# Eight chunks of gathered rows fetched row by row from SyncE, and count rows fetched for two nodes per transfer, in a graph network kernel

## Chip, cores and metric

One core of a Trainium2 chip runs the whole kernel. The time is the device time of one execution in microseconds, and the figure compared is the median over runs. A profiled execution adds a trace of every engine: TensorE (PE, its weight loads apart as PEld), VectorE (DVE), ScalarE (ACT), GpSimd (POOL) and SyncE (SP).

## What is computed

A residual layer on a graph of 12,500 nodes (64 features) and 200,000 edges that are sorted by their target node `dst`; `src` is random.

```python
h = relu(layernorm(x))
m = relu(concat(h[src], h[dst]) @ W1 + b1) @ W2 + b2   # 200000 edges, hidden size 128
s = segment_sum(m, dst)                                # one sum per node
out = x + s / max(count(dst), 1)
```

## The kernel before

**Tables first.** `h @ W1` splits into a part for the source and a part for the target. Until about 200 us the kernel writes both for all nodes to memory: `p_table` (source part, 128 floats, 512 bytes a row) and `q_table` (target part with the bias).

**The main loop.** Edges are cut into 391 quads of 512 edges (4 chunks of 128, one edge per partition). Two quads make a couple, and the loop of `fast()` runs over 182 couples, `m` = 0 to 181, on every engine, each in its own program order. A round is what an engine does for one `m`. For a couple:

- POOL fetches the source rows: one indirect DMA per chunk, 128 rows of `p_table` into one column block of tile `g` (L672 in `gather`), so 8 per couple. `g` is a ring of 26 quads, 13 couples. POOL waits once per two couples, on `u_psum` (couples that PE has finished), and then issues the next 16 indirect DMAs without another wait. How many quads it may be ahead shrinks by 4 every 48 quads, from 26 to 8 (`ahead`).
- ACT or DVE makes `spreads` (which target row belongs to which edge) and `member` (the reverse), from rows that SP broadcasts from `rel_table` (L556).
- PE adds the target part and the source part in PSUM tile `z`: `spread_q` (L1374) for couple m + 1, `add_rows` (L1386) for couple m. ACT applies relu (L812, `r_done`), PE sums the edges by node (`sum_edges`, L1401, `u_psum`), multiplies by `W2` (L1408, L1419) and DVE adds the result to the sums (L1100). In PE's program round m is: `add_rows(m)`, `times_w2` for couple m - 2, `dense(m)`, `spread_q(m + 1)`, `sum_edges(m)`.

**The dense nodes.** The first 28 quads belong to 68 nodes with very many edges, and are done another way. In rounds 3 to 42 a table of counts per source node is made (`tally_table`, stored by SP at L563). From round 49 to round 174 DVE multiplies, for each of 13 spans of 1024 source nodes and each of the 68 dense nodes, a PSUM tile (`turned`) with a row of counts (L1153, `product_of`), 6 or 7 products a round. SP brings each row of counts, broadcast to 128 partitions, 256 KB a time (L584, `load_tallies`), into one of 6 buffers, and waits until the product that used the buffer is done (`product_done`). In SP's program the rows for DVE's round m - 2 stand in round m.

**SP's program order** in a round is: `rel_table` rows (even rounds), the windows of `q_table` (L551, whose address comes from `base_i` through registers, L460), the rows of counts, and at a few rounds rows of `p_table` for a new span or stored results. A wait in it holds back all that stands behind it.

Of the kernel before, what the change touches and what calls it, by code (L numbers as in the profile page):

```python
# [8 lines left out]
I32 = mybir.dt.int32  # L9
# [153 lines left out]
BUFFERS = 6  # L163
# [30 lines left out]

MEAN_AT_OF = [BLOCK_END[k] + 2 for k in MEAN_BLOCK]
# [3 lines left out]
assert DENSE <= BT * NP and MEAN_AT_OF[0] < COUPLES  # L199
# [7 lines left out]
def gnn_kernel(nc, x, src, dst, W1, b1, W2, b2, out):  # L207
# [6 lines left out]
    with ctx:  # L214
# [60 lines left out]
        base_i = sb("base_i", [1, QT * 128], I32)  # L275
# [32 lines left out]
        tally_row = [above_ring(512 * k, 512, U16) for k in range(BUFFERS)]  # L308
        product = [above_ring(512 * k, 512, BF16) for k in range(BUFFERS)]
        p_rows = above_ring(3072, 1024, F32).rearrange("p (j h) -> p j h", h=HID)  # L310
# [69 lines left out]
        tally_in = [sem(f"tally_in{k}") for k in range(BUFFERS)]  # L380
# [71 lines left out]

        def rows_landed(m):

            rounds, k = divmod(m, RING // 2)
            return 128 * (rounds - (2 * k < RAW)) + 16 * chunks_in(m)
# [41 lines left out]
        def _(sp):  # L498
# [80 lines left out]
            def load_tallies(i, k, d):  # L579
                if i >= BUFFERS:  # L580
                    sp.wait_ge(product_done, i - BUFFERS + 1)
                row = HIGH_DIGITS * d + SPAN // 512 * k
                digits = -(-span_of(k) // 512)
                sp.dma_start(tally_row[i % BUFFERS][:, 0:512 * digits],  # L584
                             tally_table[row:row + digits, :].rearrange("(o a) b -> o (a b)", o=1)
                             .to_broadcast([128, 512 * digits])).then_inc(tally_in[i % BUFFERS], 16)
# [49 lines left out]
        def _(pool):  # L636
# [22 lines left out]
            def gather(n):  # L659
# [11 lines left out]
                for j in range(chunks_of(n)):  # L671
# [212 lines left out]
        def _(dve):  # L884
# [173 lines left out]
            nc.vector.tensor_copy(base_i[:, :], base[0:1, :]).then_inc(windows, 1)  # L1058
# [190 lines left out]
        def _(pe):  # L1249
# [318 lines left out]
```

## Time and profile before

| | |
|---|---|
| median of 3 runs | 2845.76 us (2832.94 to 2848.27) |
| profiled execution | 2839.25 us |
| its span | 2837.4 us |
| around the span | 1.85 us |
| busy: PE, DVE, POOL, ACT | 1548.3, 1428.9, 1372.7, 1189.8 us |
| mean granted TensorE clock | 0.75 of full |
| before the main loop | about 200 us |

The span runs from the first to the last instruction. No engine is busy more than 55% of it, so busy time alone does not tell what sets the time: the waits do. In every view, time stands in microseconds from the start of the span; `[11.06 <-PE bank L1401]` behind an instruction means that its engine was idle 11.06 us before it and that PE's line 1401 released it. "issue" means that nothing the profile shows was waited for, "remote" that the releaser was not found.

### The profile page before, as it was taken

Reading aid. Unit: us, or ns where it says so; the run is one execution under the profiler, and the core shown is the slowest. Engines: PE = TensorE matmul, PEld = TensorE weight load, DVE = VectorE, ACT = ScalarE, POOL = GpSimd, SP = SyncE. Lnnn points to the kernel's source line nnn. Section 1 sums busy time; section 2 is a strip of 40 time slices with the busy share of each in tenths; the row PEclk is TensorE's granted clock in tenths of the full one; section 3 lists DMA queues with packets and bytes.
Section 4 is the critical chain, followed back from the end, with each engine's and each line's share of the span. In section 5 each row is a group of like instructions: output and inputs, shape, how many; then the busy total and the mean of one; then the engine's idle time right before and its main releaser. Section 6 shows DMA issues by size and latency. Waiting matters only on the chain.

```text
span 2837.4 us, 26976 instructions
## 1 busy us (share of the span) xinstructions
PE 1548.3 (55%) x8249; PEld 1183.2 (42%) x8250; DVE 1428.9 (50%) x3051; ACT 1189.8 (42%) x2414; POOL 1372.7 (48%) x1460
## 2 busy tenths in 40 slices
PE   1656565566465564455544555455455545555556
PEld 0545353444344443344433444344344434434444
DVE  3554343343324665456655666456565556655421
ACT  1223343444314544345444454344344444444444
POOL 6345545445555445444554435545544554554553
PEclk6878777788787777677776777767776777776778
DMA  4532222222134656556565566556565665665541
GB/s 90 163 109 60 59 61 59 60 59 58 58 98 144 202 181 189 167 169 200 179 192 154 178 188 200 186 159 183 184 192 168 186 191 174 183 186 157 174 119 43
DMA packets 258990, 408.46 MB, mean 144 GB/s; under 512 B 45128, under 2 KB 118749, under 8 KB 258841
## 3 DMA queue, kind: packets, MB, share of 16 engines
q1 hardware_dynamic: 211845, 312.84, 35.7%
q0 software_dynamic: 46432, 93.61, 12.5%
q8 instruction: 68, 1.11, 0.2%
q14 instruction: 81, 0.66, 0.1%
q10 hardware_dynamic: 564, 0.23, 0.0%
HBM read 388.12 MB, written 18.38 MB: 143 GB/s over the span
## 4 chain that ended last, share of the span: by engine, by line
PE 48%; issue 36%; another core or an unknown queue 9%; DVE 6%; ACT 1%; DMA 0%; DVEq 0%; SPq 0%; ACTq 0%
PE z L1374 16%; PE bank L1401 12%; PE z L1386 10%; DVE g L1153 4%; PE bank L1419 2%; PE bank L1408 2%; PE z L1445 2%; PE bank L1430 1%; PE z L1461 1%; DVE rows_b L936 1%; PE bank L1268 1%; DVE norms L920 1%; PE z L1268 1%; ACT g L812 0%
## 5 line engine op out<-in xcount | busy, mean ns | idle before, releaser
L672 POOL DMA_INDIRECT g<-p_table,src_e x1403 | 1326.1, 945 | 1425.3 <-PE bank L1401 960.5
L1153 DVE SCALAR_TENSOR_TENSOR g<-z,norms,g 128x1024 bf16<-128x1024 f32 (+1 forms) x884 | 1019.1, 1214 | 43.5 <-issue 25.3
L812 ACT ACTIVATE g<-z 128x1024 f32<-128x1024 f32 x182 | 185.6, 1020 | 1468.0 <-remote 1153.5
L1100 DVE TENSOR_TENSOR acc<-acc,bank 65x128 f32 x191 | 54.2, 284 | 1201.0 <-remote 1069.7
L1374 PE MATMUL z<-work 128*128 128x128 f32 x1464 | 258.8, 348 | 514.2 <-issue 482.9
L1374 PE MATMUL z<-w,work 128*128 128x128 f32 x1438 | 251.9, 345 | 484.3 <-issue 443.8
L1374 PEld LDWEIGHTS z<-work 128*128 128x128 f32 x1464 | 240.3, 256 | 546.0 <-issue 541.7
L1374 PEld LDWEIGHTS z<-w,work 128*128 128x128 f32 x1438 | 234.4, 253 | 512.3 <-issue 509.3
L1401 PE MATMUL bank<-work,g 128*128 128x128 f32 x2902 | 423.4, 307 | 15.4 <-issue 15.1
L1401 PEld LDWEIGHTS bank<-work,g 128*128 128x128 f32 x2902 | 414.1, 227 | 16.8 <-issue 16.7
L1386 PE MATMUL z<-g,ident 128*128 128x512 f32 x726 | 350.8, 605 | 5.8 <-issue 5.7
L803 ACT ACTIVATE work<-columns,rel_e 128x128 f32<-128x128 f32 x1059 | 324.2, 396 | 0.0
L1386 PEld LDWEIGHTS z<-g,ident 128*128 128x128 f32 x726 | 126.0, 194 | 98.7 <-issue 98.7
L796 ACT ACTIVATE work<-work 128x1024 f32<-128x1024 f32 (+1 forms) x168 | 146.5, 872 | 4.2
L808 ACT ACTIVATE work<-work 128x1024 f32<-128x1024 f32 (+1 forms) x133 | 140.0, 1053 | 4.2
L825 ACT ACTIVATE g<-g,norms 128x512 bf16<-128x512 f32 x157 | 108.3, 716 | 0.0
L1445 PE MATMUL z<-g 128*125 128x512 bf16 x236 | 65.6, 409 | 70.6 <-remote 67.3
L1419 PE MATMUL bank<-sums_u,w 128*64 128x128 f32 (+1 forms) x312 | 78.7, 326 | 33.3 <-issue 33.3
L830 ACT ACTIVATE g<-g 128x512 bf16<-128x512 bf16 x157 | 93.5, 620 | 0.0
L1408 PE MATMUL bank<-ident,count 128*1 128x128 f32 x432 | 74.5, 273 | 9.5 <-issue 9.4
L1408 PEld LDWEIGHTS bank<-ident,count 128*1 128x1 f32 x432 | 23.4, 81 | 128.3 <-issue 125.2
L788 ACT ACTIVATE work<-rel_q,rows_f 128x1024 f32<-128x1024 bf16 (+1 forms) x67 | 75.3, 1124 | 0.0
(161 smaller groups left out, 1063.6 us busy)
## 6 DMA issues: line engine op xcount, KB each, us to landing
g<-tally_table SPq DMA_DIRECT2D x816, 256.0 KB
rel_q<-rel_table SPq DMA_DIRECT2D x46, 512.0 KB
rows_b<-rel_table SPq DMA_DIRECT2D x45, 512.0 KB
g<-p_table,src_e POOLq DMA_INDIRECT x1403
g<-tally_table SPq DMA_DIRECT2D x68, 128.0 KB
work<-q_table SPq DMA_DIRECT2D x96, 64.0 KB
w<-q_table SPq DMA_DIRECT2D x96, 64.0 KB
g<-p_table SPq DMA_DIRECT2D x12, 512.0 KB
```

Source lines behind the costliest of these rows:

```text
L672: nc.gpsimd.indirect_dma_start(out=g[:, slot(n), j * HID:(j + 1) * HID], out_offset=None, in_=p_table, in_offset=bass.IndirectOffsetOnAxis ...
L796: nc.scalar.activation(to, to, ACT.Relu, bias=1.0, scale=-1.0, accum_out=count[:, j:j + 1])\
L803: last = nc.scalar.activation(member[:, m % 2, c, :], columns[:, :], ACT.Abs, bias=rel_e[:, NC + 8 * m + c:NC + 8 * m + c + 1], scale=-1.0)
L808: nc.scalar.activation(to, to, ACT.Relu, bias=1.0, scale=-1.0)
L812: nc.scalar.activation(rows_of_p(m), z[:, 0:HID * chunks_in(m)], ACT.Relu).then_inc(r_done, 1)
L1153: nc.vector.scalar_tensor_tensor(product[i % BUFFERS][:, 0:w], turned[:, 0:w], minus_q[:, d:d + 1], tally_row[i % BUFFERS][:, 0:w], ALU.ma ...
L1374: last = nc.tensor.matmul(z[:, at:at + HID], spreads[m % 2][:, at:at + 128], qw[i % WINDOWS], start=c == 0, stop=False)
L1386: last = nc.tensor.matmul(z[:, 512 * (n % 2):512 * (n % 2) + w], ident[:, :], g[:, slot(n), 0:w], start=False, stop=True)
L1401: last = nc.tensor.matmul(u_bank[k % 2][:, at:at + WIN], g[:, slot(n), HID * c:HID * (c + 1)], member[:, m % 2, 4 * (n % 2) + c, :], start ...
L1408: nc.tensor.matmul(v[FEAT:FEAT + 1, at:at + WIN], count[:, j % COUNTS:j % COUNTS + 1], ident[:, :], start=j == parts[0], stop=j == parts[-1])
L1419: nc.tensor.matmul(v_of(k)[0:FEAT, 0:w], w2[:, :], sums_u[:, k % 2, 0:w], start=True, stop=True).then_inc(v_psum, 1)
L1445: last = nc.tensor.matmul(tally_bank[i % 2][0:125, :], high_hot[p % TALLY_PLACES], low_hot[p % TALLY_PLACES], start=p == TALLY_FIRST[i], s ...
```

## The change

Two things are changed, both in what SP issues.

**Rows of P one by one.** For eight couples (26, 46, 66, ..., 166) POOL no longer fetches the last chunk of the couple's second quad. SP does: it loads the 128 source numbers of that chunk at the start of `fast()` (eight small transfers and one wait), and in rounds c - 10 to c of couple c it loads 12 numbers into registers and issues 12 transfers of one row of 512 bytes each (8 in the last round). Before the first of a chunk it waits until couple c - 13, which used the same place of the ring, is finished by PE. PE's `add_rows` of the eight couples waits for these rows too. POOL's indirect DMAs in the main loop fall from 1347 to 1339 in the program; SP's program grows from 800 to 3095 rows of the listing below.

**Count rows in pairs.** One transfer brings the rows of counts of two nodes (512 KB); 442 in place of 884. The buffers grow from 6 to 8, and DVE waits on one semaphore for a pair. SP issues a pair for products i and i + 1 when product i - 7 is done. Where rows of P are issued too, they stand between the pairs.

SP's program where the main loop starts; before:

```order
L467 TENSOR_LOAD widest [waits q_pad,q_out3,windows,q_out2,widest_done,q_out1,q_out0]
L467 ISA x2
L468 COMPARE_AND_BRANCH
L556 DMA rel_q<-rel_table 128x2048 [waits rel_out]
L460 TENSOR_LOAD base_i
L551 ISA
```

and after:

```order
L498 TENSOR_LOAD widest [waits q_pad,q_out3,windows,q_out2,widest_done,q_out1,q_out0]
L498 ISA x2
L499 COMPARE_AND_BRANCH
L623 DMA base_i<-in_src_dram 1x128x1 x2
L623 DMA base_i<-in_src_dram 1x128 x6
L587 DMA rel_q<-rel_table 128x2048 [waits row_src_in,rel_out]
L491 TENSOR_LOAD base_i
```

Eight transfers and a wait for their landing (`row_src_in`) now stand ahead of the first row of `rel_table`.

SP's program in round 76, in the stage with products; before:

```order
L556 DMA rel_q<-rel_table 128x2048 [waits spread_done]
L460 TENSOR_LOAD base_i
L551 ISA [waits zq_done]
L551 DMA work<-q_table 128x128
L584 DMA g<-tally_table 128x1024 [waits product_done] x7
```

and after, where `u_psum` waits for couple 73:

```order
L587 DMA rel_q<-rel_table 128x2048 [waits spread_done]
L491 TENSOR_LOAD base_i
L582 ISA [waits zq_done]
L582 DMA work<-q_table 128x128
L632 TENSOR_LOAD base_i [waits u_psum]
L614 DMA g<-tally_table 128x2x1024 [waits product_done]
L642 ISA
L642 DMA g<-p_table 1x128
L642 ISA
L642 DMA g<-p_table 1x128
```

All rows of counts of the round, which stood behind `product_done` alone, now stand behind a wait for PE; 12 row transfers, each with an instruction that sets its address, are spread between them.

The core of the diff:

```diff
-BUFFERS = 6
+BUFFERS = 8
+ROW_FIRST, ROWS_EARLY, ROWS_LATE = 16, 12, 12
+def row_chunks():
+    m, chunks = ROW_FIRST, []
+    while True:
+        rows, rounds = 0, []
+        while rows < 128:
+            more = min(ROWS_EARLY if m < PRODUCT_ROUND else ROWS_LATE, 128 - rows)
+            rounds.append((m, range(rows, rows + more)))
+            rows, m = rows + more, m + 1
+        if m >= COUPLES - 1:
+            return chunks
+        chunks.append((m - 1, rounds))
+        m += 9
...
+        two_rows = [above_ring(1024 * k, 1024, U16).rearrange("p (d s) -> p d s", d=2) for k in range(BUFFERS // 2)]
...
+        def gathers_in(n):
+            return chunks_of(n) - (couple_of(n) in ROW_COUPLES and n == couple(couple_of(n))[-1])
...
             def load_tallies(i, k, d):
                 if i >= BUFFERS:
-                    sp.wait_ge(product_done, i - BUFFERS + 1)
...
+                    sp.wait_ge(product_done, i - BUFFERS + 2)
+                w = 512 * -(-span_of(k) // 512)
+                sp.dma_start(two_rows[i % BUFFERS // 2][:, :, 0:w],
...
+            def load_row_src(i):
...
+                sp.dma_start(row_src[i], edges[c:c + 1, :], allow_slow_non_contiguous=n < 128).then_inc(row_src_in, 16)
+            def row_nodes(m):
+                if m not in ROW_AT:
+                    return []
+                i, rows = ROW_AT[m]
+                if rows[0] == 0:
+                    sp.wait_ge(u_psum, ROW_COUPLES[i] - RING // 2 + 1)
+                _, nodes = nc.values_load_multi_w_load_instructions(
...
+            def load_node_rows(m, nodes):
+                for p, node in nodes:
...
+                    sp.dma_start(g[p:p + 1, slot(n), HID * c:HID * (c + 1)], p_table[bass.ds(node, 1), :])\
+                        .then_inc(row_in[i % 2], 16)
             def dense(m):
+                nodes = row_nodes(m)
...
-                for k, d in products_in(m - 2):
+                twos = [(k, d) for k, d in products_in(m - 2) if d % 2 == 0]
+                for j, (k, d) in enumerate(twos):
                     load_tallies(DENSE * k + d, k, d)
+                    load_node_rows(m, nodes[len(nodes) * j // len(twos):len(nodes) * (j + 1) // len(twos)])
+                if not twos:
+                    load_node_rows(m, nodes)
...
             def fast():
                 stores = 0
+                for i in range(len(ROW_CHUNKS)):
+                    load_row_src(i)
                 sp.wait_ge(rel_out, 16)
+                sp.wait_ge(row_src_in, 16 * len(ROW_CHUNKS))
...
-                for j in range(chunks_of(n)):
+                for j in range(gathers_in(n)):
...
-                dve.wait_ge(tally_in[i % BUFFERS], 16 * (i // BUFFERS + 1))
+                dve.wait_ge(tally_in[i % BUFFERS // 2], 16 * (i // BUFFERS + 1))
...
+                if m in ROW_COUPLES:
+                    i = ROW_COUPLES.index(m)
+                    pe.wait_ge(row_in[i % 2], 16 * 128 * (i // 2 + 1))
```

## Rows read from the trace of the kernel before

**Rows 1.** The page, part 5 (busy, mean ns, idle before): POOL's indirect DMAs.
```profile
L672 POOL DMA_INDIRECT g<-p_table,src_e x1403 | 1326.1, 945 | 1425.3 <-PE bank L1401 960.5
```
**Rows 2.** The waits, longest first: us in total, times, longest us.
```profile
ACT g L812 <- remote: 1153.5, 83, 15.6
DVE acc L1100 <- remote: 1069.7, 82, 21.7
...
POOL g L672 <- PE bank L1401: 960.5, 84, 27.9
...
POOL g L672 <- issue: 400.8, 1315, 0.3
...
DVE g L1153 <- DMA g<-tally_table: 13.1, 17, 1.6
```
**Rows 3.** The timeline, 1213 to 1247 us: start, us, engine, line.
```profile
1213.76 0.94 POOL L672 DMA_INDIRECT g<-p_table,src_e  x1 [11.06 <-PE bank L1401]
1215.01 0.94 POOL L672 DMA_INDIRECT g<-p_table,src_e  x1 [0.30 <-issue]
...
1232.48 0.94 POOL L672 DMA_INDIRECT g<-p_table,src_e  x1 [0.30 <-issue]
1236.56 1.02 ACT L812 ACTIVATE g<-z 128x1024 f32<-128x1024 f32 x1 [14.49 <-remote]
...
1237.45 1.28 DVE L1153 SCALAR_TENSOR_TENSOR g<-z,norms,g 128x1024 bf16<-128x1024 f32 x1 [0.46 <-issue]
...
1237.68 3.75 PE L1374 MATMUL z<-work 128*128 128x128 f32 x16 [15.11 <-issue]
...
1241.22 2.96 PE L1401 MATMUL bank<-work,g 128*128 128x128 f32 x16
...
1244.46 0.94 POOL L672 DMA_INDIRECT g<-p_table,src_e  x1 [11.03 <-PE bank L1401]
```
**Rows 4.** The timeline of PE inside a burst of gathers, 2761 to 2770 us.
```profile
2761.91 0.27 PE L1401 MATMUL bank<-work,g 128*128 128x128 f32 x1 [1.74 <-issue]
...
2769.69 0.59 PE L1401 MATMUL bank<-work,g 128*128 128x128 f32 x2 [1.73 <-issue]
```
**Rows 5.** Busy time by stretch; behind POOL's: granted clock, DMA share, GB/s.
```profile
1212.70:1226.20 13.50, 9.38 (x55) 6.00 (x54) 10.77 (x19) 6.76 (x14) 9.44 (x10) 1.00 0.86 262
1226.30:1243.30 17.00, 5.62 (x26) 5.65 (x27) 6.13 (x10) 6.68 (x14) 5.60 (x6) 0.50 0.34 104
```
**Rows 6.** The timeline of POOL: first gather of six bursts that follow one another.
```profile
2323.06 0.94 POOL L672 DMA_INDIRECT g<-p_table,src_e  x1 [11.06 <-PE bank L1401]
...
2352.24 0.94 POOL L672 DMA_INDIRECT g<-p_table,src_e  x1 [9.51 <-PE bank L1401]
...
2382.07 0.94 POOL L672 DMA_INDIRECT g<-p_table,src_e  x1 [10.16 <-PE bank L1401]
...
2412.33 0.94 POOL L672 DMA_INDIRECT g<-p_table,src_e  x1 [10.58 <-PE bank L1401]
...
2442.83 0.94 POOL L672 DMA_INDIRECT g<-p_table,src_e  x1 [10.82 <-PE bank L1401]
...
2473.40 0.94 POOL L672 DMA_INDIRECT g<-p_table,src_e  x1 [10.89 <-PE bank L1401]
```
**Rows 7.** The timeline of SP: a transfer of one row, and the loop's start.
```profile
22.41 0.25 SPq L506 DMA_DIRECT2D acc<-in_src_dram  x1
...
201.16 0.37 SPq L556 DMA_DIRECT2D rel_q<-rel_table  x1
```
**Rows 8.** The timeline of all engines at the loop's start: DVE.
```profile
204.56 1.28 DVE L1081 TENSOR_SCALAR_CACHE_REDUCE work<-rel_q,rows_f 128x1024 f32<-128x1024 bf16 x1 [0.94 <-DMA rel_q<-rel_table]
```
**Rows 9.** The timeline of SP, round 76 with its neighbours.
```profile
1217.89 0.43 SPq L556 DMA_DIRECT2D rel_q<-rel_table  x1
...
1219.47 5.61 SPq L584 DMA_DIRECT2D g<-tally_table  x6
...
1238.77 9.77 SPq L584 DMA_DIRECT2D g<-tally_table  x7
```
**Rows 10.** The waits of SP's queue: us in total, times, longest us.
```profile
SPq L584 <- DVE g L1153: 1048.0, 441, 14.9
```

More of the change, by code:

```diff
@@ L192, in span_of @@
     return SPAN if k < SPANS - 1 else TAIL
+ROW_FIRST, ROWS_EARLY, ROWS_LATE = 16, 12, 12
[11 more added lines that the diff above has]
+        m += 9
+ROW_CHUNKS = row_chunks()
+ROW_COUPLES = [m for m, _ in ROW_CHUNKS]
+ROW_AT = {m: (i, rows) for i, (_, rounds) in enumerate(ROW_CHUNKS) for m, rows in rounds}
+assert len(ROW_CHUNKS) <= 24 and ROW_COUPLES[0] >= RING // 2
 MEAN_AT_OF = [BLOCK_END[k] + 2 for k in MEAN_BLOCK]
@@ L198 @@
     MEAN_AT_OF[0] += 1
-assert DENSE <= BT * NP and MEAN_AT_OF[0] < COUPLES
+assert DENSE % 2 == 0 and DENSE <= BT * NP and MEAN_AT_OF[0] < COUPLES
 ORDER = sorted(range(BATCHES), key=lambda b: MEAN_AT_OF[b])
@@ L274, in gnn_kernel @@
         base = sb("base", [128, QT * 128])
-        base_i = sb("base_i", [1, QT * 128], I32)
+        base_i = sb("base_i", [128, QT * 128], I32)
+        places = [(k, q) for k in (base_i, real[:, :].bitcast(I32)) for q in (32, 64, 96)]
+        row_src = [k[q:q + 1, 128 * i:128 * (i + 1)] for k, q in places for i in range(4)]
         idx_raw = sb("idx_raw", [128, 4 * RAW], I32)
@@ L308, in gnn_kernel @@
         tally_row = [above_ring(512 * k, 512, U16) for k in range(BUFFERS)]
+        two_rows = [above_ring(1024 * k, 1024, U16).rearrange("p (d s) -> p d s", d=2) for k in range(BUFFERS // 2)]
         product = [above_ring(512 * k, 512, BF16) for k in range(BUFFERS)]
-        p_rows = above_ring(3072, 1024, F32).rearrange("p (j h) -> p j h", h=HID)
+        p_rows = above_ring(512 * BUFFERS, 1024, F32).rearrange("p (j h) -> p j h", h=HID)
         parts_d = norms[:, 0:SPANS * DENSE].rearrange("p (d k) -> p d k", k=SPANS)
@@ L379, in gnn_kernel @@
             "p_rows_in turned_done product_done edges_psum added_done v_dense_psum dense_added dense_range")
-        tally_in = [sem(f"tally_in{k}") for k in range(BUFFERS)]
+        row_src_in = sem("row_src_in")
+        row_in = [sem(f"row_in{k}") for k in range(2)]
+        tally_in = [sem(f"tally_in{k}") for k in range(BUFFERS // 2)]
         o_psum, most_done, inverse_done, mean_done, out_done = sems("o_psum most_done inverse_done mean_done out_done")
@@ L451, in rows_of_p @@
             return g[:, k:k + 2, :].rearrange("p k c -> p (k c)")[:, 0:HID * chunks_in(m)]
+        def gathers_in(n):
+            return chunks_of(n) - (couple_of(n) in ROW_COUPLES and n == couple(couple_of(n))[-1])
         def rows_landed(m):
-            rounds, k = divmod(m, RING // 2)
-            return 128 * (rounds - (2 * k < RAW)) + 16 * chunks_in(m)
+            first = m % (RING // 2) + (RING // 2 if 2 * (m % (RING // 2)) < RAW else 0)
+            return 16 * sum(gathers_in(n) for c in range(first, m + 1, RING // 2) for n in couple(c))
         def first_nodes(eng, n):
@@ L580, in load_tallies @@
                 if i >= BUFFERS:
-                    sp.wait_ge(product_done, i - BUFFERS + 1)
[L582 to L586, printed above, removed]
+                    sp.wait_ge(product_done, i - BUFFERS + 2)
+                w = 512 * -(-span_of(k) // 512)
+                sp.dma_start(two_rows[i % BUFFERS // 2][:, :, 0:w],
+                             tally_table.rearrange("(o d a) b -> o d (a b)", o=1, a=HIGH_DIGITS)[:, d:d + 2, SPAN * k:SPAN * k + w]
+                             .to_broadcast([128, 2, w])).then_inc(tally_in[i % BUFFERS // 2], 16)
+            def load_row_src(i):
+                n = couple(ROW_COUPLES[i])[-1]
+                at, c = n * QE, chunks_of(n) - 1
+                edges = src[at:at + QE].rearrange("(e c) -> c e", c=4) if n < 128 else \
+                    src[at:at + QE].rearrange("(c e) -> c e", c=4)
+                sp.dma_start(row_src[i], edges[c:c + 1, :], allow_slow_non_contiguous=n < 128).then_inc(row_src_in, 16)
[6 more added lines that the diff above has]
+                _, nodes = nc.values_load_multi_w_load_instructions(
+                    row_src[i][:, rows[0]:rows[-1] + 1], engines=[sp.engine], min_val=0, max_val=NODES - 1,
+                    skip_runtime_bounds_check_because="src holds nodes")
+                return list(zip(rows, nodes))
+            def load_node_rows(m, nodes):
+                for p, node in nodes:
+                    i = ROW_AT[m][0]
+                    n = couple(ROW_COUPLES[i])[-1]
+                    c = chunks_of(n) - 1
+                    sp.dma_start(g[p:p + 1, slot(n), HID * c:HID * (c + 1)], p_table[bass.ds(node, 1), :])\
+                        .then_inc(row_in[i % 2], 16)
             def dense(m):
+                nodes = row_nodes(m)
                 if m == TALLY_ROUND - 3:
@@ L1057, in _ @@
             nc.vector.tensor_copy(spans_i[:, :], bank[1][0:1, :]).then_inc(span_done_i, 1)
-            nc.vector.tensor_copy(base_i[:, :], base[0:1, :]).then_inc(windows, 1)
+            nc.vector.tensor_copy(base_i[0:1, :], base[0:1, :]).then_inc(windows, 1)
             for t in range(QT):
```

## Prediction

> **What bounds the kernel now.** I read the page's costliest groups first, then the waits, then the timeline of one cycle. POOL's indirect DMAs are 1326.1 us busy, 945 ns each, with 1425.3 us idle before them [rows 1]. The waits say that both sides wait: POOL waited 960.5 us in 84 waits for PE's `sum_edges`, and ACT's relu waited 1153.5 us, 83 times, for a release that was not found [rows 2]. About 84 long waits in 182 couples is one per two couples, so the timeline of two couples is the thing to see [rows 3]. POOL starts a burst of 16 gathers at 1213.76; starts are 1.25 us apart (945 ns and 0.30 of issue), and the last begins at 1232.48 and ends at 1233.42, so a burst is 19.66 us. ACT's relu of couple 73 (counted from the first of L812) begins at 1236.56, 3.14 us after the burst's end, having waited 14.49. Then comes PE: `spread_q` of couple 74 from 1237.68 (3.75 us), `sum_edges` of couple 73 from 1241.22 (2.96 us), and at 1244.46 POOL is released into its next burst. The cycle is 19.66 + 3.14 + 7.90 = 30.70 us.
>
> What PE waits for in it is not the burst's data: the burst that starts at 1213.76 fetches couples 79 and 80 by the count of L672. PE simply comes forward very little while POOL issues. In one late burst, where PE has nothing else to wait for, its matmuls stand singly with gaps of about 1.7 us [rows 4], where 16 of them take 3 us outside. Why is not shown; that the two take turns is. So POOL's gather time is on the path nearly whole, although POOL is idle half of the time. DVE and SP are not on it: DVE waited 13.1 us for count rows in all [rows 2], and SP waited 1048.0 us for DVE's products [rows 10].
>
> **The change, part by part.**
>
> *Eight gathers fewer on POOL.* Each takes 1.25 us out of a burst (15 in place of 16): 8 x 1.25 = 10.0 us. Nothing hides a burst's end, so I take all of it; the ends are 0 (something restores the cycle) and what follows.
>
> *The clock.* In a cycle the granted clock is at 2.4 GHz for the stretch around the burst's start and at 1.2 GHz from its middle until the next one is near (1.00 and 0.50) [rows 5]; PE had been idle before it fell and had worked for some us before it rose. PE's 6.7 us after a burst are mostly done at the low level. A cycle that comes out early is followed by more short ones: the burst at 2352.24 came 29.18 us after the one before, the next after 29.83, 30.26, 30.50 and 30.57, where 30.70 is usual [rows 6]. The shortfalls are 1.52 + 0.87 + 0.44 + 0.20 + 0.13 = 3.16 us, so a cycle early by 1.52 us gave 1.64 more in the cycles behind it. A burst shorter by 1.25 us then gives 1.6 more (the same sequel) to 1.9 (the same total). I expect it in the stage of products, where the cycles are steady and six of the eight chunks lie, and not in all of them: 4 x 1.6 to 4 x 1.9 = 6.4 to 7.6 us, taken 7. The ends are 0 and 8 x 1.9 = 15.
>
> *The start.* Eight small transfers and the wait for their landing stand ahead of the first row of `rel_table`, which is issued at 201.16 [rows 7], and DVE waited for its landing until 204.56 [rows 8]: it is on the path, nothing covers it. A transfer of one row took SP 0.25 us to issue [rows 7], with the gap 0.3; two of the eight pick single numbers and may take 0.5. That is 2.8 us of issue, and the landing of the last is bounded by the 3.4 us from issue to use of the first `rel_table` rows (4.56 - 1.16, a far larger transfer) and 1 us. Sum +3.8 to +6.2, taken +4.8.
>
> *1024 row transfers on SP.* Each has an instruction for its address. By the row of 0.25 us and two gaps and the register work (0.15) it costs 0.42 us of SP: 12 are 5.0 us a round. The trace has no one-row transfer with a register address; the nearest from above are the windows of `q_table` at 0.56 us [rows 9], so 6.7 us. A round lasts 30.7 / 2 = 15.4 us, and SP now waits 1048.0 us over 126 product rounds, 8.3 us a round [rows 10]. It fits, and costs 0 on the path. If it did not, SP would be late with count rows, which is the second rival.
>
> *The wait for couple c - 13 ahead of a chunk.* Behind it on SP stand the count rows of that round and all later ones. Round 76's are issued from 1219.47 [rows 9] for products that start at 1237.45 [rows 3]; now they wait for couple 73, whose `sum_edges` ends at 1244.2. With a load of registers (0.6) and about 3 us to land, DVE's round 74 starts at 1248, 10.5 us late, six times. Who waits: `add_sums` behind those products, and PE's `times_w2` behind that, which stands in round 75 inside the next burst, where PE stands still until 1267. DVE waited 1069.7 us in 82 waits at `add_sums` [rows 2], 13 us a cycle, so 10.5 fits, narrowly. Cost 0, at most 3 us in the two chunks (146, 166) whose waiting couple is released in mid cycle: 0 to +6, taken +2. The first two chunks have no count rows behind the wait: 0. The last rows of a chunk are issued in SP's round c. Round 76 was issued by 1225.08 [rows 9], and PE's `add_rows(76)` stands behind the relu of couple 75, one cycle after 1236.56: 42 us of lead, so the wait on the rows themselves costs 0.
>
> *Count rows in pairs.* 442 issues of 0.33 to 0.5 us in place of 884 of 0.37: SP gains about 1 us a round, the bytes are the same. The first product of a pair needs 512 KB landed, but it is requested six products (7.3 us) ahead as before. DVE waited 13.1 us for count rows in all, so at best that much is won on an engine with slack: 0.
>
> A page of the Trainium skill, "DMA: Bandwidth & Descriptors", section "Rules for kernel authors", speaks against this: many small transfers are to be coalesced, since below 64 KB the overhead is most of what is paid, and section "Anatomy of one DMA" gives about 2.0 us fixed for each. Laid end to end that would be an estimated 24 us a round of 12 rows, over the 15.4 of a round, and the chunks' 88 rounds would add some 760 us. The trace speaks for overlap: six transfers of 256 KB were issued in 5.61 us [rows 9], so I give a serial landing of the rows a chance of 0.01.
>
> Sum against the profiled execution (2839.25, of which 1.85 lies around the span): - 10.0 - 7 + 4.8 + 2 = - 10.2, so 2829.1. The median shown is 6.5 us above that execution; the middle of all four times is 2842.5, which would give 2832.3. I say **2831**.
>
> **Rivals.**
>
> *B, the burst is shorter and nothing else comes of it.* If the cycle falls back to 30.70 after each, only the direct 10.0 is left: - 10.0 + 4.8 + 2 = - 3, so 2838 to 2840. For it: most cycles are 30.7 whatever small work is in them, and six rows of one event are all I have for the follow-up.
>
> *C, no gain at all.* PE's progress after a burst may hang on the clock's next rise and not on the burst's end; then a burst that ends 1.25 us sooner changes nothing. + 4.8 + 2 over the base: 2847. For it: the cycle is very regular, POOL's idle time before its bursts is 11.06, 11.03 and again 11.06 us [rows 3, 6]. Against it: the shortfalls of rows 6. The same page of the Trainium skill (section "Issuing engines are not separate DMA queues") says that moving a transfer to another engine saves only the sequencer's time, since all run on the same 16 DMA engines. By it nothing is won but POOL's own 1.25 us; rows 3 say that this is just the time PE waits for.
>
> *D, slower: SP comes too late with the count rows.* The mechanism: the wait for couple c - 13, then 12 rows a round, make DVE late by more than the 13 us it idles, and PE waits for DVE at `times_w2` and at the change of a span. It decides at about 0.7 us a row: round 76 would then need 8.4 + 3 us, DVE's two rounds would end at about 1270, past 1267, and the lateness comes back each cycle of the chunk until SP has its lead again. Price: 3 to 5 us in each of six chunks at the start and 1 us in each of 5 cycles, 6 x 9 = 54 at worst, 30 as its likely size: 2842.5 - 10 + 4.8 + 30 = 2867. For it: 0.56 us on some rows of `q_table`. Against it: 0.25 for the one-row transfer.
>
> **How the numbers follow.** Forecast 0.42, B 0.24, C 0.15, D 0.16, something else 0.03 (the serial landing in it). The forecast's own range is 2818 to 2838: all gains at their upper ends, 2842.5 - 10 - 15 + 3.8 = 2821, and from the profiled execution 2818; without most of the sequels 2838. To leave out no more than 2 in 10, the range goes from 2816 over B and C to the near end of D: 2816 to 2858. A measurement of this kernel can tell about 0.5% from no change, 14 us: below 2831.5 is faster, above 2860 slower. About half of the forecast's spread lies below 2831.5, but both times come from the same session and the base may be lower: faster 0.38, same 0.45, slower 0.17.
>
> **What would show it.** Right: eight bursts with 15 gathers, 1.25 us shorter, in the timeline of POOL; the cycle after them below 30.7; DVE's first operation on the rows of `rel_table` at 209 in place of 204.56; PE's `add_rows` of the eight couples without a wait of its own; row transfers on SP of 0.3 us each; POOL's wait for PE about unchanged. Wrong: cycles of 30.7 with 15 gathers and a longer pause after them (C); DVE waiting for count rows tens of us in all, or PE's `times_w2` later than the relu it used to precede (D); a loop start that has not moved, which would give 5 us back.

## The result, and the profile after

The changed kernel takes 2904.76 us (median; 2898.61 to 2907.78), the kernel before 2845.85 in the same session: a ratio of 1.021, 95% interval 1.019 to 1.0231. The forecast was 2831. The change costs 59 us.

The groups of the page and the waits, of the kernel after (rows 1, 2 and 10 are those of before; L737 was L672, L1218 was L1153, L1469 was L1401, L614 was L584):

```profile
L737 POOL DMA_INDIRECT g<-p_table,src_e x1395 | 1319.3, 946 | 1498.4 <-PE bank L1469 1032.4
```

```profile
ACT g L877 <- remote: 1115.8, 79, 18.5
POOL g L737 <- PE bank L1469: 1032.4, 83, 40.9
...
DVE acc L1165 <- remote: 708.3, 55, 22.2
DVE g L1218 <- DMA g<-tally_table: 445.3, 89, 23.0
```

POOL issues eight gathers fewer and is 6.8 us less busy, but its idle time has grown by 73.1 us. The wait that has appeared is DVE's for count rows: 445.3 us in 89 waits, where it was 13.1 in 17 [rows 2]. Most of it came out of DVE's old idle time (1069.7 to 708.3), but not all of it. The next fence is SP's queue (issue times; a row's transfer is L642):

```profile
SPq L614 <- DVE g L1218: 427.0, 141, 15.4
...
SPq L632 <- PE bank L1469: 161.1, 6, 32.3
```

SP waits 621 us less for DVE than before [rows 10], though the new wait for couple c - 13 takes only 161.1 of that in the product stage. Most of the rest is SP's own time on the rows. SP's timeline of the fourth chunk, inside a burst that runs from 1299.73 to 1319.4, and then outside one (start, us, engine, line, transfers):

```profile
1302.39 4.48 SPq L642 DMA_DIRECT2D g<-p_table  x4
1306.88 0.70 SPq L614 DMA_DIRECT2D g<-tally_table  x1
1309.74 11.25 SPq L642 DMA_DIRECT2D g<-p_table  x4
1322.38 0.00 SPq L582 DMA_DIRECT2D w<-q_table  x1
...
1333.03 1.54 SPq L642 DMA_DIRECT2D g<-p_table  x4
1334.62 0.40 SPq L614 DMA_DIRECT2D g<-tally_table  x1
1335.21 1.46 SPq L642 DMA_DIRECT2D g<-p_table  x4
```

Four rows take 1.5 us outside a burst and, in the middle of one, over 11. The view of the line tells why. It lists the three instructions of a row, with the shortest, median and longest duration in ns:

```profile
L642 SPq FUSED_REGOPS  x1024: 2/37/1395, 403.1 to 2657.7; - x171
L642 SPq MOVE g<-p_table x1024: 1/29/1387, 403.2 to 2657.8; - x171
L642 SPq DMA_DIRECT2D g<-p_table x1024: 1/228/1396, 403.3 to 2657.8; - x171
```

A register addition and a move have nothing to wait for. Normally they take 37 and 29 ns; inside a burst most take 0.70 us or near nothing (339 and 256 of 691), like the other SP instructions there: SP comes forward by about one instruction per 0.70 us. This begins some 3 us behind the burst's first gather and ends some 3 us behind its last, which is about when the relu begins that waits for PE [rows 3]. Counted over the trace, some 290 of the 1024 rows lie inside such a stretch and cost SP 2.2 us each (mean, start to start of what follows); the others cost 0.45 (median 0.41). The mean is 0.95.

What it leads to, in the order of the chain (all engines, 1327 to 1361 us):

```profile
1327.56 1.28 DVE L1218 SCALAR_TENSOR_TENSOR g<-z,norms,g 128x1024 bf16<-128x1024 f32 x1 [13.56 <-DMA g<-tally_table]
...
1345.84 1.94 PE L1529 MATMUL z<-ident,g 128*128 128x128 f32 x8 [7.52 <-DVE g L1218]
...
1355.04 1.02 ACT L877 ACTIVATE g<-z 128x1024 f32<-128x1024 f32 x1 [15.88 <-PE z L1454]
...
1360.25 0.94 POOL L737 DMA_INDIRECT g<-p_table,src_e  x1 [40.85 <-PE bank L1469]
```

DVE waits 13.56 us for count rows that SP issued late, PE waits for DVE's product at the change of a span (L1529), the relu comes late, and POOL's burst starts 60.5 us after the one before, where 45.3 is usual at that place (there POOL skips a burst). Four more such gaps, each in another chunk and ahead of a burst's first gather (11.0 is usual, 9.5 to 10.9 behind a short cycle):

```profile
1055.43 0.94 POOL L737 DMA_INDIRECT g<-p_table,src_e  x1 [20.48 <-PE bank L1469]
...
1672.77 0.95 POOL L737 DMA_INDIRECT g<-p_table,src_e  x1 [18.77 <-PE bank L1469]
...
2256.91 0.94 POOL L737 DMA_INDIRECT g<-p_table,src_e  x1 [21.04 <-PE bank L1469]
...
2574.35 0.94 POOL L737 DMA_INDIRECT g<-p_table,src_e  x1 [21.67 <-PE bank L1469]
```

Burst by burst against the trace before: nine long cycles in the product stage, less one short one, cost 63.5 us together (15.2 at most, at 1360.25), the first burst comes 9.8 us later (233.01 against 223.22), the stage before the products adds 7.8, and the short bursts give back 14.6 in the product stage. That is 66.5, the difference of the two spans (2903.9 and 2837.4).

### The profile page after: what moved, and what is told of

It is laid out like the page before. It is cut to its first block, busy times and chain, and to the rows that moved or that the text cites. A ratio compares the mean times of both kernels' runs of the same rounds, so it can differ in the third digit from the quotient of the medians.

```text
span 2903.9 us, 29703 instructions
## 1 busy us (share of the span) xinstructions
PE 1580.4 (54%) x8249; PEld 1192.1 (41%) x8250; DVE 1430.4 (49%) x3051; ACT 1190.1 (41%) x2414; POOL 1365.9 (47%) x1452
## 4 chain that ended last, share of the span: by engine, by line
PE 33%; issue 33%; another core or an unknown queue 11%; SPq 10%; DVE 7%; DMA 5%; ACT 2%; DVEq 0%; ACTq 0%
PE z L1439 11%; PE bank L1469 8%; SPq L642 7%; PE z L1454 7%; DMA g<-tally_table 5%; DVE g L1218 4%; PE z L1513 2%; PE bank L1476 1%; PE bank L1487 1%; SPq L614 1%; SPq L582 1%; SPq L632 1%; DVE rows_b L1001 1%; DVE norms L985 0%
## 5 line engine op out<-in xcount | busy, mean ns | idle before, releaser
L737 POOL DMA_INDIRECT g<-p_table,src_e x1395 | 1319.3, 946 | 1498.4 <-PE bank L1469 1032.4
L1218 DVE SCALAR_TENSOR_TENSOR g<-z,norms,g 128x1024 bf16<-128x1024 f32 (+1 forms) x884 | 1023.8, 1214 | 493.6 <-DMA g<-tally_table 445.3
L1439 PE MATMUL z<-w,work 128*128 128x128 f32 x1438 | 263.0, 356 | 387.5 <-issue 345.3
L1165 DVE TENSOR_TENSOR acc<-acc,bank 65x128 f32 x191 | 53.9, 282 | 791.8 <-remote 708.3
L1439 PEld LDWEIGHTS z<-w,work 128*128 128x128 f32 x1438 | 245.2, 264 | 415.0 <-issue 411.6
L1469 PE MATMUL bank<-work,g 128*128 128x128 f32 x2902 | 406.3, 299 | 15.3 <-issue 15.1
L1469 PEld LDWEIGHTS bank<-work,g 128*128 128x128 f32 x2902 | 396.5, 218 | 16.3 <-issue 16.3
L1454 PE MATMUL z<-g,ident 128*128 128x512 f32 x726 | 360.4, 618 | 9.4 <-issue 9.0
L1513 PE MATMUL z<-g 128*125 128x512 bf16 x236 | 73.1, 421 | 103.2 <-remote 64.2
L1513 PEld LDWEIGHTS z<-g 128*125 128x125 bf16 x236 | 32.7, 145 | 137.1 <-issue 128.4
```

What stands on the lines that cost most here:

```text
L737: nc.gpsimd.indirect_dma_start(out=g[:, slot(n), j * HID:(j + 1) * HID], out_offset=None, in_=p_table, in_offset=bass.IndirectOffsetOnAxis ...
L1218: nc.vector.scalar_tensor_tensor(product[i % BUFFERS][:, 0:w], turned[:, 0:w], minus_q[:, d:d + 1], tally_row[i % BUFFERS][:, 0:w], ALU.ma ...
L1439: last = nc.tensor.matmul(z[:, at:at + HID], spreads[m % 2][:, at:at + 128], qw[i % WINDOWS], start=c == 0, stop=False)
L1454: last = nc.tensor.matmul(z[:, 512 * (n % 2):512 * (n % 2) + w], ident[:, :], g[:, slot(n), 0:w], start=False, stop=True)
L1469: last = nc.tensor.matmul(u_bank[k % 2][:, at:at + WIN], g[:, slot(n), HID * c:HID * (c + 1)], member[:, m % 2, 4 * (n % 2) + c, :], start ...
L1513: last = nc.tensor.matmul(tally_bank[i % 2][0:125, :], high_hot[p % TALLY_PLACES], low_hot[p % TALLY_PLACES], start=p == TALLY_FIRST[i], s ...
```

## The experiments

Many of the runs met something that the two recorded sessions had not shown: there the kernel before took 1847 us, not 2846. In other runs it took 2825 to 2849 again. There are two conditions, with no time in between, and each experiment is compared only with the kernel before on the same chip in the same session. Below they are called the long condition (2846) and the short one (1847).

### The short condition: what it is

*r1_after* is the changed kernel, unaltered.

> The changed kernel again. The runs of the first eight experiments took 1848 us with the kernel before, where the recorded comparison had 2846, and in them every SP instruction took its normal time (0.03, 0.04, 0.23 us) inside the gathers too. Theory S (two conditions of the machine: in one, engines take 0.70 us an instruction while gathers move, in the other not; rows cost the change its time only in the first): if the kernel before takes about 1848 us here, the changed kernel takes 1840 to 1845, by fixed_address (1844.8) and src_later (1838.5); if it takes about 2846, the changed kernel takes 2900 to 2910 as recorded. Rival R (the rows cost the change 59 us whatever the condition): 1900 beside 1848.

Measured: 1843.57 against 1846.03, ratio 0.9982 (0.997 to 0.9994). The program is the same, and here the change is 0.2% faster. Its trace: the page's group of gathers, the view of L642, and two rows of PE from a stretch in which POOL issues gathers throughout:

```profile
L737 POOL DMA_INDIRECT g<-p_table,src_e x1395 | 1318.3, 945 | 442.2 <-issue 423.5
```

```profile
L642 SPq FUSED_REGOPS  x1024: 37/37/42, 236.1 to 1663.7; - x171
L642 SPq MOVE g<-p_table x1024: 29/29/37, 236.2 to 1663.7; - x171
L642 SPq DMA_DIRECT2D g<-p_table x1024: 224/228/1018, 236.2 to 1663.8; - x171
```

```profile
1309.55 1.95 PE L1439 MATMUL z<-work 128*128 128x128 f32 x16
1311.33 1.95 PE L1469 MATMUL bank<-work,g 128*128 128x128 f32 x16
```

The gathers take the same 945 ns, but no register instruction of SP is stretched (42 ns at most; 10 of the 1024 row issues take over 0.30 us), and PE does 16 matmuls in 1.95 us beside the gathers. POOL never pauses in the loop: its idle time is the issue gap of 0.30 us. The pace of single matmuls is not what tells the conditions apart, though. In the trace before, PE keeps the same pace for the first part of a burst, here the one from 1213.76 to 1233.42:

```profile
1216.37 2.02 PE L1374 MATMUL z<-work 128*128 128x128 f32 x16 [0.49 <-issue]
...
1218.22 1.95 PE L1401 MATMUL bank<-work,g 128*128 128x128 f32 x16
```

Its last matmul there ends 8.8 us behind the first gather, and the next comes at 1237.68, 15.11 us later [rows 3]; half of the bursts of the product stage look like this. In the short condition PE's longest idle time in that stage is 7.6 us. So the 1000 us between the conditions, the bursts, the pauses and the 30.7 us cycle go together with whether PE and SP come forward to the end of a run of gathers. That this one thing makes all the rest is my reading; no run shows it apart.

*r0_before* is the kernel before, unaltered.

> The kernel before, to have its trace in the condition of these runs. If its time is about 1847 us: SP's and PE's instructions take the same time inside the gathers as outside, POOL issues a gather every 1.25 us from the loop's start to the end without a wait for PE's sum_edges, and no relu waits 14 us. If it is about 2846, the bursts of 16 and the pauses of 11 us are there.

It met the long condition: 2828.6 against 2825.42 (ratio 1.0006, 0.9985 to 1.0026). Its bursts are those of rows 3 and 6, in another session than the recorded trace.

### The parts of the change in the long condition

*s3_fewer_gathers* leaves out all that SP does for the rows; the rows of the eight chunks are wrong in the sums (PE adds what was left in the ring).

```
-    sp.wait_ge(row_src_in, ...); load_row_src(i)          # the start
-    sp.wait_ge(u_psum, ROW_COUPLES[i] - RING // 2 + 1)
-    load_node_rows(...), pe.wait_ge(row_in[i % 2], ...)
```

> The kernel of fewer_gathers again (eight gathers fewer, nothing on SP for them, their rows of the sum left out), for the condition in which the kernel before takes about 2840 us. By the short bursts of no_rows (the cycle behind one is 2.4 us shorter and those that follow together another 1) it is 8 x 2.4 to 8 x 3.4 below the kernel before, 19 to 27 us; by rival B of the prediction 10; by rival C nothing.

Measured: 2824.28 against 2842.46, ratio 0.9938 (0.9914 to 0.9962), 18 us. The first gathers of a burst with 15 gathers (2246.45) and of the three behind it:

```profile
2246.45 0.95 POOL L729 DMA_INDIRECT g<-p_table,src_e  x1 [11.00 <-PE bank L1458]
...
2274.83 0.95 POOL L729 DMA_INDIRECT g<-p_table,src_e  x1 [9.91 <-PE bank L1458]
...
2305.07 0.94 POOL L729 DMA_INDIRECT g<-p_table,src_e  x1 [10.51 <-PE bank L1458]
...
2335.54 0.95 POOL L729 DMA_INDIRECT g<-p_table,src_e  x1 [10.77 <-PE bank L1458]
```

The cycle with the short burst is 28.38 us and the next two 30.24 and 30.47, against 30.70: 2.32 + 0.46 + 0.23, 3.0 us for one gather. The burst itself is 1.25 shorter; another 1.1 comes off the pause behind it at once, the rest in the next cycles. That is just under what was expected. Rival C of the prediction falls; rival B's 10 us lie just below the interval of 11 to 24, and the cycles rule it out.

*s2_no_rows* keeps the eight small transfers ahead of the loop and the wait for couple c - 13, and leaves out the row transfers and their register loads.

> The kernel of no_rows again (no row transfers, nothing in the chunks; their rows of the sum are wrong) for the condition in which the kernel before takes about 2840 us. Theory T: the gathers' gain of 20 to 28 less 4 to 9 at the start and 0 to 6 for the wait, 2815 to 2840. Rival W (the wait alone makes DVE late): 2870 or more.

Measured: 2831.51 against 2849.02, ratio 0.9939 (0.9914 to 0.9964). Nothing is lost against fewer_gathers that these intervals could show. The wait does what was worked out: it makes DVE late, and that stays in DVE's slack.

```profile
DVE g L1215 <- DMA g<-tally_table: 98.3, 18, 22.3
```

That is 98.3 us in 18 waits, up to 22.3, against 15.6 in 11 without the wait for the couple (fewer_gathers). Rival W falls.

*s2_fixed_address* has all 1024 row transfers, of the same size, at the same places, with the same waits and loads of node numbers, but from an address that is known when the program is built. The fetched rows are the wrong ones.

```
-  sp.dma_start(g[...], p_table[bass.ds(node, 1), :])
+  sp.dma_start(g[...], p_table[128 * i + p:128 * i + p + 1, :])
```

> As s1_fixed_address, which met the condition of 1847 us: where the kernel before takes about 2840 us, theory T gives 2835 to 2870, rival M 2880 to 2910.

Measured: 2837.25 against 2849.02, ratio 0.9957 (0.9936 to 0.9979). This is the run that settles it. DVE waits 120.5 us for count rows where the changed kernel had 445.3. A row is now one instruction, and inside a burst three rows take 2.83 us with their gaps (0.66 us a row as a mean over the bursts, 0.29 outside, 0.46 over all):

```profile
DVE g L1218 <- DMA g<-tally_table: 120.5, 26, 22.3
```

```profile
1347.27 2.83 SPq L642 DMA_DIRECT2D g<-p_table  x3
1350.80 0.70 SPq L614 DMA_DIRECT2D g<-tally_table  x1
```

The same transfers with two register instructions less each are 71 us faster against their own kernel before (59 above, 12 below). Between this run and no_rows lie 6 us, which the intervals of some 7 hardly tell from none: that is what the transfers themselves cost. Rival M falls: it is not bandwidth, not the queue, not the landing of small transfers. What costs the time is the two register instructions of each row on SP, which the bursts stretch. One thing more differs in this run and was not tried alone: its rows lie next to each other in the table, where the right ones are scattered.

*s3_src_later* issues the eight small transfers of node numbers in rounds 5 to 12 in place of ahead of the loop.

```
-  for i in range(len(ROW_CHUNKS)): load_row_src(i)      # ahead of the loop
+  if 5 <= m < 5 + len(ROW_CHUNKS): load_row_src(m - 5)
+  if m == ROW_FIRST - 1: sp.wait_ge(row_src_in, 16 * len(ROW_CHUNKS))
```

> The kernel of src_later again (the eight small transfers in rounds 5 to 12), for the same condition. Theory T: it is the changed kernel less 4.3 us of its start, so 50 to 60 us above the kernel before, with 0.70 us steps of SP inside the gathers.

Measured: 2899.91 against 2842.46, ratio 1.0209 (1.0169 to 1.0248), where the changed kernel has 1.021. DVE waits 439.7 us for count rows, as in the changed kernel. Its first burst starts at 226.24 in place of 233.01, so the start was 6.8 us earlier, and the end shows none of it.

*s3_pairs* has the count rows in pairs and eight buffers, and no row chunks.

```
-ROW_CHUNKS = row_chunks()
+ROW_CHUNKS = []
```

> The kernel of pairs again (count rows in pairs, no row chunks), for the same condition. Theory T: within 10 us of the kernel before. Rival P (the 512 KB landings cost part of the 59 us): 20 us or more above it.

Measured: 2841.04 against 2842.46, ratio 1.001 (0.9993 to 1.0027); DVE waits 10.6 us for count rows. Pairs are free, and rival P falls.

### The same edits in the short condition

> The change without its row chunks: count rows in pairs and eight buffers, all gathers on POOL as in the kernel before. Theory T (the 59 us come from SP, which needs 0.70 us for every instruction while a burst's gathers move, and a row is three instructions; pairs of count rows cost nothing): within 5 us of the kernel before, 2841 to 2851, DVE waits for count rows 10 to 20 us in all. Rival P (a product now waits for 512 KB in place of 256, and SP may ask for the next pair only when two products are done): most of the 445 us that DVE waited for count rows are here too, 2870 or more.

> The changed kernel without the 1024 row transfers and the register work for them; the chunks are not filled, so 8 x 128 rows of the sum are wrong. The eight small transfers ahead of the loop, the wait for couple c - 13 on SP and the eight dropped gathers stay. Theory T: the eight cycles keep their gain (2.5 us each and about 1 us in the cycles behind, 20 to 28 in all), the start costs 4 to 9, the wait 0 to 6: 2825 to 2840, DVE waits for count rows under 100 us. Rival W (it is the wait, up to 32 us long with all later count rows behind it, that makes DVE late): 2870 or more, with DVE's waits for count rows at 300 us or more.

> The kernel with count rows in pairs and eight gathers fewer on POOL, and nothing on SP for them: no rows, no wait, no small transfers at the start (8 x 128 rows of the sum are left out). It measures what eight gathers are worth. Theory T: 8 x 2.5 plus the shorter cycles behind, 20 to 30 us below the kernel before, 2816 to 2826. Rival B of the prediction (the direct 1.25 us each and no more): 2836. Rival C (no gain): 2846.

> The changed kernel with the same 1024 row transfers, each from a fixed row of the table, so that a row is one instruction on SP in place of three (the fetched rows are the wrong ones; loads of the node numbers and all waits stay). Theory T: inside a burst a row costs SP 0.7 us in place of 2.1 to 2.8, 12 rows 8.4 in place of 25 to 34; DVE waits for count rows under 200 us in place of 445, and the time is 2835 to 2870. Rival M (the small transfers themselves hold up the queue or the DMA engines, and so the count rows): the bytes, the transfers and their number are unchanged, so 2895 to 2910.

Measured, against 1849.87: pairs 1849.31 (ratio 0.9995, 0.9985 to 1.0005), no_rows 1844.21 (0.997, 0.9957 to 0.9984), fewer_gathers 1838.51 (0.9937, 0.9918 to 0.9956), fixed_address 1844.75 (0.9967, 0.9955 to 0.9978). The times that the theories gave were for a kernel before of 2846 and do not apply; the differences do. Eight gathers are worth 11.4 us here, nearly the direct 8 x 1.25. Fixed addresses are worth nothing that shows against the changed kernel's 0.9982: where no register instruction is stretched, three instructions a row cost the kernel no more than one. A second run of fixed_address, meant for the long condition, met the short one and gave 0.9979 (0.9968 to 0.9991).

> The kernel of fixed_address again (each row from a fixed place, one SP instruction in place of three; the fetched rows are the wrong ones), for the condition in which the kernel before takes about 2840 us. Theory T there: DVE waits for count rows under 200 us in place of 445, 2835 to 2870. Rival M (the small transfers themselves hold up the count rows): 2880 to 2910. Where the kernel before takes 1847 us it only repeats 1845.

*e6_src_later*, the edit shown above, and *e2_rows*, the row chunks with one count row per transfer and six buffers:

> The changed kernel with the eight small transfers of node numbers issued one a round in rounds 5 to 12 in place of ahead of the loop, and waited for in round 15. Theory T: they held the first rows of rel_table by 4.3 us (205.21 to 209.47), so 2898 to 2902. If the loop starts no earlier (the other 4 us of its delay were there before SP came to them) the time is 2903 to 2907.

> The changed kernel with its row chunks, but with one count row per transfer and six buffers, as before the change. Theory T: SP has 442 instructions more, some of them inside bursts at 0.70 us, and a smaller lead: 2905 to 2925. Rival P (pairs are to blame): 2880 or less.

```
-BUFFERS = 8
+BUFFERS = 6
-  sp.dma_start(two_rows[...], <two rows of tally_table>)
+  sp.dma_start(tally_row[i % BUFFERS][:, 0:w], <one row>)
```

Measured against 1847.6: src_later 1838.49 (0.9955, 0.9941 to 0.9969), rows 1855.58 (1.0037, 1.0023 to 1.0051). The start is on the path here, 5 us of it: src_later is better than both kernels in the short condition, and in the long one as slow as the changed kernel. Pairs, which are free without the rows, are worth some 10 us with them (1855.6 against the 1843.6 of r1_after, in two sessions). DVE's waits for count rows fit that SP has become short of time: 151.1 us with single rows, 98.8 in r1_after.

*e7_one_less* drops one gather in every second couple from couple 16 on, 83 in all (1320 on its page against 1403; the expectation counted 82), with nothing on SP for them; these rows of the sum are wrong.

```
+ROW_COUPLES = [m for m in range(16, COUPLES - 1) if m % 2 == 0]
```

> One gather fewer in every second couple from couple 16 on (82 in all), nothing on SP for them, count rows in pairs; 82 x 128 rows of the sum are left out. It measures whether the cycle of two couples follows the burst. If it follows one to one: 82 x 1.25 = 102 us, 2743. If each gives 2.5 as the single short bursts do: 205 us, 2640. If the cycle is held by the clock's next rise and stays at 30.7: 2846 and bursts of 15 with a longer pause behind.

Measured: 1754.43 against 1847.6, ratio 0.9496 (0.9465 to 0.9527), 93 us or 1.12 a gather, where its direct price is 1.25. POOL is nearly the whole path in the short condition. What 83 gathers give in the long one was not tried.

*e8_no_gathers_late* has no gather at all from couple 90 on (the rows of the sum are wrong there).

> The changed kernel without any gather from couple 90 on (rows of the sum left out there); SP still loads its rows in the chunks at rounds 96 to 166. What counts is the time of an SP instruction there. Theory T (it is POOL's gathers that slow the other engines' sequencers): row transfers, moves and register additions take 0.23, 0.03 and 0.04 us in all later chunks, no 0.70 us steps, and a row costs 0.40 us. Rival (SP's own small transfers fill its queue): the 0.70 us steps stay. The time falls by some hundred us either way.

Measured: 1782.64 against 1847.6, in one run. No register instruction of SP was stretched in it, but none is in the short condition with gathers either, so it says nothing on its question. It fell by 65 us only, not hundreds: without gathers DVE's products, 1.2 us each and seven a couple, are next in line (DVE is busy 558.8 of the 600 us from 1000 to 1600).

### The dose

If SP's time per row decides, it must do so in the short condition too, once a row costs enough. *n1_two_parts* and *n2_four_parts* split each row into two and four transfers, with the same bytes.

```
+  for part in range(0, HID, HID // 2):      # HID // 4 in n2_four_parts
+      sp.dma_start(g[p:p + 1, slot(n), ...], p_table[bass.ds(node, 1), part:part + HID // 2])
```

> The changed kernel with each row in two transfers of 256 bytes: the same rows and bytes, but SP needs about 0.8 us a row in place of 0.40. Theory D (what decides is SP's time per row against the length of a round): where the kernel before takes 1848 us a round is 9.7 us; 12 rows then take 9.6 and the rest of a round some 3.5, so SP falls behind by 3.4 us a round, 38 us in a chunk against a lead of about 30, and DVE is late by some 10 us in each of six chunks: 1865 to 1905, DVE's waits for count rows 150 us or more. If rows cost nothing but at their landing, 1844. Where the kernel before takes 2846, a row inside a burst costs twice as much too and the time is above 3000.

> The changed kernel with each row in four transfers of 128 bytes, about 1.6 us of SP a row. Theory D, where the kernel before takes 1848 us: 12 rows take 19.2 us in a round of 9.7, so SP falls behind by 13 us a round, 140 us in a chunk less 30 of lead, in six chunks: 2300 to 2600. If the time follows the bytes, 1844.

Measured: 2124.05 against 1847.58 (1.1487, 1.1466 to 1.1508) and 2975.49 against 1845.08 (1.611, 1.6014 to 1.6207). A part costs SP 0.41 us, so a row 0.82 and 1.64. The waits of the first:

```profile
DVE g L1220 <- DMA g<-tally_table: 368.7, 235, 5.0
...
POOL g L739 <- PE bank L1471: 310.4, 43, 38.5
```

The mechanism is that of rival D and stronger than I put it. Twelve rows of 0.82 are 9.8 us; count rows (four transfers of 0.44), the load of the node numbers (0.95) and the rest (0.8) make some 3.5 more, and a round lasts 9.7. That is 3.6 us too much in each of the 66 product rounds with rows, and 1.6 in the 22 earlier ones, which have no count rows: 273 us, and 276 were measured. With four parts it is 19.7 + 3.5 - 9.7 = 13.5 and 11.5, 1144 us; 1130 were measured. By stage the sum fits less well: the first product comes 65 us later than in r1_after where the sum says 35, and the stage of products is 218 longer where it says 238; with four parts these are 277 (253) and 860 (891). I had let SP's lead of 30 us pay for part of it, six times over. By this sum it pays nothing; that the wait for couple c - 13 has already used the lead up when a chunk begins is my explanation and was not measured. Nor do these two runs tell SP's instructions from the number of transfers, since both grow together; only fixed_address does.

## Why the prediction was wrong, point by point

- **The gathers** (- 10 and - 7): right. 17 was the sum, 18.2 was measured. The direct part is 1.25 and the sequel 1.8, where I took 1.6 to 1.9. It came in five of the six product chunks where I counted four (in the fourth the next cycle is 0.7 us shorter and little of that stays), and more of it at once. That the sums agree so closely is in part luck.
- **Pairs of count rows** (0): right.
- **The start** (+ 4.8): too small as a delay, and not seen at the end. SP's eight transfers are issued from 205.21 and the first row of `rel_table` at 209.47, 4.26 us, within the 3.8 to 6.2 of the forecast:

```profile
205.21 3.23 SPq L623 DMA_DIRECT2D base_i<-in_src_dram  x8
209.47 0.37 SPq L587 DMA_DIRECT2D rel_q<-rel_table  x1
```

  But that is 8.31 us later than before. Another 2.7 come from the table, which is stored at 199.07 in place of 196.40, and 1.4 lie between that and the eight transfers; no run explains them. DVE's first operation stands at 213.32, not at 209:

```profile
213.32 1.28 DVE L1146 TENSOR_SCALAR_CACHE_REDUCE work<-rel_q,rows_f 128x1024 f32<-128x1024 bf16 x1 [5.70 <-DMA rel_q<-rel_table]
```

  In the long condition the end does not show it: no_rows, with the transfers and the wait, lies within 1 us of fewer_gathers by their ratios, with intervals of some 7 us. In the two traces its bursts come 6.9 us later at the first, 16.6 in mid loop (one starts at 1573.55 and 1556.98) and 9.7 near the end, so what the start costs there stays open. In the short condition 5 us show.
- **The wait for couple c - 13** (+ 2): right as far as the intervals tell. It makes DVE later than the 10.5 us worked out (SP waits up to 32.3 us, DVE up to 22.3 in no_rows), and the time stays.
- **The rows on SP** (0): this is the step that failed. "12 are 5.0 us a round ... It fits, and costs 0 on the path." The 0.42 us is right outside a burst (0.41). Inside one, where SP spends 19.7 of each 30.7 us, it is 2.2, five times as much, and the mean of 0.95 is above the point of 0.7 us a row that I had worked out for rival D. Twelve rows at 0.95 are 11.4 us a round, where SP had 8.3 to spare [rows 10]; so it does not fit, and the term that was put at nothing is the largest of all. Against no_rows the rows cost 76 us with three instructions each (59 and 17.5, from two sessions), and some 6 with one.
- **Rival D**, with 0.16, is what came. Its place (count rows late, then the change of a span) and its chain were right, and its threshold of 0.7 us a row lies between the 0.46 of fixed_address and the 0.95 of the changed kernel. Its price of 30, at worst 54, was short.

What I had in hand: the trace before shows six count-row transfers in 5.61 us inside a burst [rows 9]. I took the row as proof that they overlap, and it says little on either side: the first two take 0.64 and 0.71 us, where an issue takes 0.32 elsewhere, and the last four take 0.32 but start 1.20 apart, at the pace of DVE's products that free the buffers. And I wrote of PE that it "comes forward very little while POOL issues", and did not ask whether SP does the same. The trace before says so in one more view, that of L551, where the same two register instructions stand for the windows of `q_table`:

```profile
L551 SPq FUSED_REGOPS  x192: 5/37/701, 202.2 to 2780.2; - x192
L551 SPq MOVE work<-q_table x96: 6/29/708, 202.2 to 2749.3; - x96
```

The median of 29 ns hid the longest of 708, and a row's cost is in the longest. Only 26 of the 162 register instructions inside bursts are stretched in that trace, 339 of 691 in the changed kernel's. The page of the Trainium skill that I weighed ("DMA: Bandwidth & Descriptors", against many small transfers) pointed to the right side for another reason: the transfers are nearly free, as fixed_address shows; their addresses are not. Its 2.0 us fixed is given for transfers issued from GpSimd, and these are issued from SP; the estimated 760 us of a serial landing did not come.

## What to carry to other kernels

Where one engine stands still while another issues gathers, suspect the others' queues too until the trace says otherwise: look at the longest duration of the cheapest instruction (a register move) on each queue, not at the median. Cost work that is moved to a queue in instructions, at the rate of the worst stretch that it will lie in, and ask what else waits in that queue. And a lead that one edit may use up (a new wait at the head of a chunk) should not be counted on to pay for the next.

## What the runs showed of the hardware

The same program takes 1847 us or 2846. The gathers take 945 ns in both. In the long condition SP's instructions can go forward by only one per 0.70 us while gathers are under way, and PE stops some 9 us into most bursts, or comes forward one matmul per 1.7 us [rows 4]; in the short one neither is seen. The operations themselves are not longer: PE's 16 matmuls take 1.95 us and DVE's products 1.28 us beside gathers in both conditions. The mean granted TensorE clock is 0.75 in the long condition and 0.91 in the short one, and PE is busy 55% and 78% of the span. I don't know what makes the condition. Runs in which the chip had the same number in the records met the short one in one session and the long one in another, so it is not a property of the chip's number alone. That gathers cause the stretching is not shown. It rests on coincidence: in the traces of the changed kernel and the one before, every stretched register instruction lies between 2.3 us behind a burst's first gather and 3.1 behind its last; the run that took the gathers away met the short condition, and a kernel with other traffic in their place was not tried.

In the long condition none of the kernels that fetch the right rows beats the kernel before; in the short one the changed kernel does by 0.2% and src_later by 0.45%.
